# Gated delta-rule attention in a two-layer block on one NeuronCore: projections, solve, gated output and inverse steps placed anew within a loop step

## What is computed

```python
qkvz = hidden_states @ W_qkvz                 # per key head: q, k, 2 v, 2 z
conv = silu(sum(xp[:, j:j + Tv, :] * conv_w[:, j] for j in range(4)))   # q, k, v
beta, alpha = sigmoid(b), exp(-exp(A_log) * softplus(a + dt_bias))
q = l2norm(q) * DK ** -0.5;  k = l2norm(k)
def step(S, inp):                             # S: 128 x 128 per value head
    S = S * a_t
    v_new = (v_t - k_t @ S) * b_t
    S = S + outer(k_t, v_new)
    return S, q_t @ S
og = o * silu(z)
og = og * rsqrt(mean(og * og) + 1e-6) * norm_weight
out = og @ W_out                              # added to x, scaled by a gate
```

## Time and profile before

| | |
|---|---|
| median of 3 runs | 1607.65 us (1607.57 to 1608.58) |
| profiled execution, its time | 1606.35 us |
| its span, first to last instruction | 1604.6 us |
| mean granted TensorE clock over the span | 0.844 |
| busy share of the span: PE, DVE, ACT, POOL | 82%, 59%, 50%, 43% |

### The profile page before, as it was taken

How to read it: one execution, slowest core, us unless ns; L and a number is a source line. 1 busy time by engine, 2 the same in 40 slices (tenths; PEclk the granted TensorE clock), 3 DMA queues, 4 the chain that set the end, 5 groups by cost and what they waited for, 6 DMA issues and landing times. The chain is left out here.

```text
span 1604.6 us, 29952 instructions
## 1 busy us (share of the span) xinstructions
PE 1322.6 (82%) x10580; PEld 1120.7 (70%) x10580; DVE 954.1 (59%) x2298; ACT 809.6 (50%) x2096; POOL 690.4 (43%) x1137
## 2 busy tenths in 40 slices
PE   4376889889898988989889798898877399799995
PEld 1265778778787877878778787787766245488883
DVE  2487577786867868677686777768121322343335
ACT  1333466666666666665665666666453130353431
POOL 0118466485665746657475664856440000100000
PEclk8577799999999999999999999999776599855556
DMA  3311312313122130211303122021020300000002
GB/s 107 96 29 37 82 30 65 69 27 87 28 67 41 52 90 20 73 35 60 88 13 82 30 65 72 23 56 29 16 52 1 116 17 0 1 1 1 1 0 82
DMA packets 145273, 73.87 MB, mean 46 GB/s; under 512 B 118708, under 2 KB 134596, under 8 KB 143076
## 3 DMA queue, kind: packets, MB, share of 16 engines
q1 hardware_dynamic: 145124, 71.96, 17.4%
HBM read 58.11 MB, written 13.78 MB: 45 GB/s over the span
## 5 line engine op out<-in xcount | busy, mean ns | idle before, releaser
L878 POOL TENSOR_TENSOR tmp<-Dm,Tn 64x31 f32<-64x31 f32 (+15 forms) x496 | 253.7, 511 | 139.1 <-DMA Dm<-blk_in_scratch 104.9
L881 POOL TENSOR_TENSOR Tn<-Tn,tmp 64x31 f32<-64x31 f32 (+15 forms) x496 | 276.0, 556 | 38.9
L727 DVE SCALAR_TENSOR_TENSOR cqk<-bank,cw,cqk 128x255 f32<-128x255 f32 (+2 forms) x384 | 155.4, 475 | 151.5 <-ACT cqk L588 151.5
L854 POOL TENSOR_TENSOR ro<-ss,mhalf 128x4 f32<-128x4 f32 x64 | 64.6, 1009 | 297.3 <-issue 223.4
L727 DVE SCALAR_TENSOR_TENSOR cv<-bank,cw,cv 128x255 f32<-128x255 f32 (+2 forms) x384 | 155.4, 475 | 30.3 <-ACT cv L588 30.2
L649 ACT ACTIVATE junk<-og 128x129 f32<-128x129 f32 x256 | 80.1, 313 | 166.1 <-DVE og L799 137.5
L522 PE MATMUL bank<-wo,OTs 128*128 128x256 f32 x512 | 156.4, 433 | 3.4 <-ACT OTs L678 3.4
L786 DVE SCALAR_TENSOR_TENSOR BP<-bank,cj,E 128x512 f32<-128x512 f32 (+1 forms) x256 | 142.8, 612 | 2.3
L380 PE MATMUL bank<-hh,wqk_hi 128*128 128x256 f32 x256 | 94.9, 371 | 26.3 <-DVE wqk_lo L745 17.4
L114 POOL TENSOR_SCALAR vare<-mv 128x8 f32<-128x8 f32 x4 | 1.0, 239 | 259.3 <-DVE mv L105 259.3
L522 PEld LDWEIGHTS bank<-wo,OTs 128*128 128x128 f32 x512 | 95.5, 207 | 23.8 <-ACT OTs L678 10.2
(11 more groups left out here) (206 smaller groups left out, 3726.4 us busy)
## 6 DMA issues: line engine op xcount, KB each, us to landing
alb<-alpha_scratch SPq DMA_DIRECT2D x8, 1024.0 KB, 6.2
rvz<-in_L_attn_W_qkvz SPq DMA_DIRECT2D x16, 512.0 KB, 5.9
x<-alpha_scratch SPq DMA_DIRECT2D x8, 1024.0 KB, 6.4
blk_in_scratch<-BP SPq DMA_DIRECT2D x512, 8.0 KB, 1.5
rqk<-in_L_attn_W_qkvz SPq DMA_DIRECT2D x16, 256.0 KB, 2.6
wo<-in_L_attn_W_out SPq DMA_DIRECT2D x16, 256.0 KB, 6.9
tinv_scratch<-Tn SPq DMA_DIRECT2D x32, 128.0 KB, 2.2
tinv_t_scratch<-Tt SPq DMA_DIRECT2D x32, 128.0 KB, 2.2
```

The lines of the kernel that those rows point to most:

```text
L727: nc.vector.scalar_tensor_tensor(dst[:, t, s:T], bk[:, t * T:(t + 1) * T - s], cw[p][:, first + t, TAPS - 1 - s:TAPS - s], dst[:, t, s:T], ...
L854: nc.gpsimd.tensor_tensor(ro[b % 2][:], ss[b % 2][:], mhalf[:, 0:4], ALU.pow).then_inc(sem("ro"), 1)
L878: pool_step_done(nc.gpsimd.tensor_tensor(t, Dm[:, j, j + 1:BLK].unsqueeze(2).broadcast_to([SLOTS, r, c]), Tn[:, j, 0:c].unsqueeze(1).broad ...
L881: pool_step_done(nc.gpsimd.tensor_tensor(Tn[:, j + 1:BLK, 0:c], Tn[:, j + 1:BLK, 0:c], t, ALU.subtract), kh * NTS + 2 * j + 4)
```

## The change

- Banks: `bank[0]` is only the q/k projection's, `bank[1]` the first Gram matrix's, `bank[2]` the second's, and v and z share `bank[3]`. `pe_v` now also waits for the silu of the z before it, `pe_z` for the convolution of the v before it. `pe_qk` waits only for the convolution before it.
- PE: a step begins with both halves of the q/k projection. In merge steps the second half of v and the transposes `pe_ot` lie between merge stages 0 and 1, and `pe_vt` between solves 1 and 2. In plain steps `pe_z` comes last.
- ACT: in plain steps `act_silu_z` and then `act_ss` of the step itself come last, and in `b` = 3 `act_turn` after them; in merge steps `act_ogn` comes ahead of merge copy 0, `act_ots` ahead of merge copy 1, and `act_silu_qk` ahead of `act_y` 0.
- DVE: the scans move from the end of a step to the start of the next one, ahead of `dve_scales`; in plain steps `dve_og` of the step itself ends the step.
- The splits move: q/k from `b` = 2 to 1, v/z from `b` = 3 to the next head's `b` = 0.
- POOL: the parts of the inverse are 4, 11, 6 and 10 pairs (before 5, 10, 10 and 6); `pool_ro` is issued at the end of its own step, which leaves its place among POOL's instructions as it was but for the parts' borders.
- The stretch ahead of the loop: z of a sequence moves one turn later, ahead of the next v; the first Gram matrices no longer borrow `bank[6]`.

```diff
-            bQK, bG2, bV, bZ, bVT, bF, bX, bO = bank
-            bG1, bOT, bU = bQK, bVT, bO
+            bQK, bG1, bG2, bV, bVT, bF, bX, bO = bank
+            bZ, bOT, bU = bV, bVT, bO
...
             def pe_qk
-                    if lead:
-                        wait(nc.tensor, "conv_qk", at(kh, b, 6))
-                    else:
-                        wait(nc.tensor, "bp", at(kh, b, 4, -2))
+                    wait(nc.tensor, "conv_qk", at(kh, b, 6))
...
             def pe_v
                     wait(nc.tensor, "conv_v", at(kh, b, 6))
+                    wait(nc.tensor, "silu_z", at(kh, b, 1))
...
             def pe_z
-                    wait(nc.tensor, "silu_z", at(kh, b, 1))
+                    wait(nc.tensor, "conv_v", at(kh, b, 6, 6))
...
             def pe_step
+                if qk:
+                    pe_qk(*qk, 0)
+                    pe_qk(*qk, 1)
                 if gram:
                     pe_gram0(*gram)
                     pe_gram1(*gram)
+                if merges(b):
+                    if vz:
+                        pe_v(*vz, 0)
+                    pe_merge(kh, p, b, 0)
+                    if vz:
+                        pe_v(*vz, 1)
+                    if last:
+                        pe_ot(*last, 2 * (now + 2))
+                    pe_merge(kh, p, b, 1)
+                    if last:
+                        pe_f(*last, 0)
+                    pe_merge(kh, p, b, 2)
+                    if last:
+                        pe_f(*last, 1)
+                    pe_merge(kh, p, b, 3)
+                    if vz:
+                        pe_z(*vz, 0)
                     pe_solve(kh, p, b, 0)
+                    if vz:
+                        pe_z(*vz, 1)
                     pe_solve(kh, p, b, 1)
+                    if vt:
+                        pe_vt(*vt, now)
                     pe_solve(kh, p, b, 2)
                     pe_o(kh, p, b, 0)
+                    pe_o(kh, p, b, 1)
+                else:
+                    pe_solve(kh, p, b, 0)
+                    if vt:
+                        pe_vt(*vt, now - 1)
+                    if vz:
+                        pe_v(*vz, 0)
+                    pe_solve(kh, p, b, 1)
+                    if vz:
+                        pe_v(*vz, 1)
+                    pe_ot(*last, 2 * (now + 3))
+                    pe_solve(kh, p, b, 2)
+                    pe_o(kh, p, b, 0)
+                    pe_f(*last, 0)
+                    pe_o(kh, p, b, 1)
+                    pe_f(*last, 1)
+                    if vz:
+                        pe_z(*vz, 0)
+                        pe_z(*vz, 1)
...
             def act_silu_z
                 wait(nc.scalar, "z_mm", at(kh, b, 1, 1))
+                wait(nc.scalar, "og", at(kh, b, 2, -6))
...
             def act_step
+                if last and merges(last[2]):
                     act_ss(*last)
...
+                    if qk:
+                        act_silu_qk(*qk)
+                    if vz:
+                        act_silu_z(*vz)
+                    act_ss(kh, p, b)
                 if b == B - 1 and exists(kh, b, 1):
                     act_turn(kh + 1)
...
             def splits
-                if b == 2 and exists(kh + 3, 0, 0):
+                if b == 1 and exists(kh + 3, 0, 0):
                     split_qk(kh + 3, 1 - p)
-                if b == 3 and exists(kh + 2, 0, 0):
-                    split_vz(kh + 2, p)
+                if b == 0 and kh and exists(kh + 1, 0, 0):
+                    split_vz(kh + 1, 1 - p)
...
             def dve_step
                 if gram:
+                    for n in range(2 * R):
+                        dve_scan(*gram, n)
                     dve_scales(*gram)
                     dve_bp(*gram, 0)
...
+                if merges(b):
                     dve_r2(kh, p, b)
-                if qk:
-                    for n in range(2 * R):
-                        dve_scan(*qk, n)
+                else:
+                    dve_og(kh, p, b)
...
-            SPLIT = {0: (0, 5), 1: (5, 15), 2: (15, 25), 3: (25, BLK - 1)}
+            SPLIT = ((0, 4), (4, 15), (15, 21), (21, BLK - 1))
```

More of the change, by code:

```diff
@@ L389, in pe_gram0 @@
                 wait(nc.tensor, "bp", at(kh, b, 4))
-                nc.tensor.matmul(g1[:], sqk[i][:, 1, 0:P], sqk[i][:].rearrange("p x t -> p (x t)"), start=True, stop=True)
+                nc.tensor.matmul(bG1[:], sqk[i][:, 1, 0:P], sqk[i][:].rearrange("p x t -> p (x t)"), start=True, stop=True)
             def pe_gram1(kh, p, b):
@@ L503, in pe_o, with pe_ot @@
                 last.then_inc(sem("o"), 1)
-            def pe_ot(kh, p, b):
+            def pe_ot(kh, p, b, scaled):
                 wait(nc.tensor, "ogn", at(kh, b, 4, 4))
-                v = at(kh, b, 2, 8)
-                wait(nc.tensor, "vs", min(v, 2 * NG) if isinstance(v, int) else v)
+                wait(nc.tensor, "vs", min(scaled, 2 * NG))
                 for h in range(R):
@@ L554, in pe_step @@
[L554 to L569, removed]
@@ L696, in act_step @@
-                if last:
-                    act_ogn(*last)
-                if merge:
-                    act_merge(kh, p, b, 1)
-                if last:
-                    act_ots(*last)
                 if qk:
                     act_tap0(*qk, "qk", bQK, cqk, 0)
-                if merge:
+                if merges(b):
+                    if last:
+                        act_ogn(*last)
+                    act_merge(kh, p, b, 0)
+                    if vz:
+                        act_tap0(*vz, "v", bV, cv, 2)
+                    if last:
+                        act_ots(*last)
+                    act_merge(kh, p, b, 1)
+                    if vz:
+                        act_silu_v(*vz)
@@ L715, in act_step @@
-                if merge:
+                    if vz:
+                        act_silu_z(*vz)
                     act_y(kh, p, b, 1)
+                    if vt:
+                        act_vs(*vt)
+                else:
+                    act_y(kh, p, b, 0)
+                    if vt:
+                        act_vs(*vt)
+                    act_ogn(*last)
+                    if vz:
+                        act_tap0(*vz, "v", bV, cv, 2)
+                    act_y(kh, p, b, 1)
+                    act_ots(*last)
+                    if vz:
+                        act_silu_v(*vz)
+                    if qk:
+                        act_silu_qk(*qk)
+                    if vz:
+                        act_silu_z(*vz)
+                    act_ss(kh, p, b)
@@ L884, in pool_step @@
             def pool_step(kh, p, b):
-                last = beside(kh, p, b, -1)
-                if last:
-                    pool_ro(*last)
                 if kh + 1 < NKH:
@@ L892, in pool_step @@
                     pool_inverse(kh + 1, *SPLIT[b])
+                pool_ro(kh, p, b)
             def sp_load_qk(kh):
@@ L1085, in _ @@
                         for c in range(NC):
-                            dve_bp(gk, gk, gb, c, bX)
-                    for n in range(2 * R):
-                        dve_scan(kh, kh, b, n)
+                            dve_bp(gk, gk, gb, c)
+                    if g < LEAD_GRAM:
+                        for n in range(2 * R):
+                            dve_scan(kh, kh, b, n)
                     if 0 <= g - B < LEAD_VZ:
```

88 lines of the change are left out of this document (25 added, 63 removed).

## The result

The changed kernel takes 1679.97 us, median of 4 runs (1678.01 to 1682.1), against 1607.61 (1604.98 to 1608.58, 4 runs) for the kernel before in the same comparison: a ratio of 1.0446, 95% interval 1.0431 to 1.0461. The forecast was 1670, slower, range 1605 to 1715. The profiled execution has a span of 1676.3 us at a mean granted clock of 0.80.

A forecast was written before the change was run, and what follows sets the result against it. PE bounds step `b` = 1; `b` = 0 loses most, waiting at merge stage 0. Steps of 26.8 + 17.8 + 14.0 + 14.0 = 72.6 against 68.2: 4.4 a head, 14 heads, 62 us, so 1670; range 1605 to 1715.

The forecast's parts named there:

- The turn and the merge: ACT's turn starts 2.65 us into `b` = 0, merge stage 0 at 10.7; PE waits 6.2 us there.
- The 6.07 from the turn's end to the merge: In `b` = 0, time from ACT's turn ending to merge stage 0, kept from before because SP's order isn't changed.
- POOL isn't the limit: Claim that POOL's inverse, ending 0.8 us into the next head's first step, doesn't hold back the turn: cost 0.
- Plain steps: The two steps without merges: 12.7 us of work and 1.3 of waits, 14.0 each, a gain of 1.3 for both.
- The waits that I named: PE's waits in a plain step: 0.5 us for `ogn` at `pe_ot`, 0.8 for `OTs` at `pe_f` 0.
- the q/k term: PE's q/k projection at the step's start: 1.6 us a pair, 0.80 a half, taken equal to v's.
- Merge steps: From merge stage 0 on 13.3 us against 12.39; `b` = 1 takes 17.8, a loss of 1.3.
- Clock in `b` = 0: Lower clock behind the merge adds 2.8 us to 13.3; the step takes 26.8, a loss of 4.4.
- the bound of 5.6 from head 14: Upper bound of the clock term in `b` = 0, from head 14's first step: 18.9 us, 5.6 over 13.3.
- low-clock rival: Rival: the stretch after the merge behaves as in head 14, 2.8 us more a head, 1709 us; chance 0.15.
- Banks, scans, splits, ends: Bank sharing by v and z, moved scans and splits, stretch ahead of the loop, last two heads: each costed at 0.
- its 2.16 for the clock: Time the kernel before loses to the low clock in `b` = 0, from the merge on: 14.55 against 12.39 us.

The follow-up runs named there:

- e1: The changed kernel with ACT's turn moved ahead of the silu of z and the sums of squares in `b` = 3: 1645.80 us.
- e2: The changed kernel with the turn ahead of silu and square of q/k, and POOL's parts 4, 11, 8, 8 pairs: 1560.96 us.
- e4: The kernel before with the turn moved behind the sums of squares of the next head's first step: 1687.29 us.
- e10: The changed kernel with v's second half done seven times more (42 matmuls, results unused) in PE's wait ahead of merge stage 0 in `b` = 0: 1607.04 us.
- e11: e9 with v's second half done twice more (12 matmuls, results written over) ahead of merge stage 0 in `b` = 0: 1502.17 us.
- e7: The changed kernel with POOL's inverse in parts of 5, 10, 10 and 6 pairs again: 1678.68 us.
- e5: e8 with the second q/k half behind merge stage 1 in merge steps, and ACT's tap of q/k behind merge copy 1: 1554.56 us.
- e6: The changed kernel with 12 more matmuls of the q/k projection's shape behind merge stage 0 in `b` = 0, results unused: 1636.52 us.
- e9: e8 with POOL's parts 5, 12, 8 and 6 pairs: 1556.15 us.
- e8: e2 with `Y` ahead of silu of q/k and of z in merge steps, and `OTs` ahead of the second `Y` in plain steps: 1563.02 us.

## Why the prediction was right, and which of its sizes were not

- *The turn and the merge* (right, shown by e1, e2 and e4). Forecast: turn at 2.65, merge at 10.7, a wait of 6.2. Measured: 2.74, 10.87 (mean 10.63), 6.37. The 6.07 from the turn's end to the merge was 6.13. The turn's own sum is written wrongly: 0.2 + 0.58 + 1.67 make 2.45, not 2.65. The silu of z started at 0.49 instead of 0.2, behind silu and square of q/k, and this hid the slip. That POOL isn't the limit held for after: its last pair ends 1.14 into the step (forecast 0.8), 1.6 ahead of the turn. But the room is small: in e1, with the turn at 1.70, it waits for POOL 1.12.
- *Plain steps* (direction right, size off by 2.0 a head). Forecast 14.0 each, measured 13.05 and 12.98. The waits that I named are there, and `Y` is in time, but they are 0.6 smaller together: `ogn` 0.22 for 0.5 and `OTs` 0.52 for 0.8. The other 0.4 is PE's work: I took 12.7 from the busy time of before, and it is 12.3. Part of it is in the q/k term: I took 0.80 a half from the v half, and 12 q/k matmuls in a row, right behind z of the same shape, take 1.44 (652.44 to 653.88).
- *Merge steps* (size nearly right). `b` = 1: forecast 17.8, measured 17.45. That is near by two errors against each other: the waits for `Y` and `R2` of 0.45 and 0.35 are not there (under 0.1), and PE is idle 0.59 instead of 1.55, but it is busy 16.86, where I had taken 16.25. From the merge on at full clock I had 13.3; e10 shows 12.95.
- *Clock in* `b` = 0 (mis-sized). Forecast 2.8 over 13.3; measured 19.22 - 12.95 = 6.3. I had the bound of 5.6 from head 14 and chose against it, because v half 1 stays behind stage 0. This head's 18.86 is the 18.9 of the low-clock rival. The total came out near the forecast (72.6 a head, measured 73.3) only because the plain steps gave 2.0 back, and that is luck; the rival's time of 1709 would have needed them at 14.0.
- *Banks, scans, splits, ends* (costed at 0). PE has no wait for the silu of z or the taps of v in the head shown, and one of 0.8 for the silu of z in the whole loop. Of the 71.7 between the two profiled spans, 13 heads make 68.2; the last two heads take 1.4 more, the rest of the program, whose code is the same, 4.5 more, and what lies ahead of the 13 heads 2.4 less.

So where did the 5.1 us a head go? e10 gives the change at full clock, in the head that starts at 359.90: 10.64 + 12.95 + 17.44 + 13.05 + 12.99 = 67.1. The kernel before without its 2.16 for the clock would be 68.2 - 2.2 = 66.0. The order of the work, with the longer wait in it, costs 1.0 a head (`b` = 0 3.3 and `b` = 1 1.0 more, plain steps 3.3 less), and the clock 6.3 - 2.2 = 4.1. Four fifths of the loss are the clock, and the late turn starts it.

The Trainium skill, "TensorE: Matmul & The Clock Gate" (HAM oscillation — how this bites in real kernels), describes a loop whose matmuls wait for a DMA, so that each burst starts at the low clock. The trace agrees: with the wait filled, 9 of 13 heads of e10 ran 12.95 and 12 of 13 of e11 12.70, at a clock of 1.00. The Trainium skill, on the same page (Part 1: The HAM clock gate), says that activity releases the throttle. Here the trace disagrees: in after PE was busy 18.76 of 18.86 us and the mean clock was 0.59.

## What to carry to other kernels

Where an engine of fixed order issues a long-latency chain, place that instruction first and move everything else around it: here its place was worth 5% of the kernel before (e4) and, with two of POOL's pairs moved, 7% of the kernel after (e2). Cost a longer wait of TensorE at the idle time plus the slower clock behind it, which was the larger part here, and ask whether independent or even repeated matmuls can fill the wait. When a shortened step brings nothing, look for the engine whose chain now closes the head (here POOL), and for what stands in the queue behind the instruction that waits for it.

## What the runs showed of the hardware

- The low clock holds while PE works: 19.44 of 19.47 us busy at a mean clock of 0.56 in e7.
- Waits of only 1.5 to 2.1 us can be followed by the low clock: in e2 the same stretch took 12.94, 13.93 or 19.37 us.
- In e5 the clock fell behind a wait of 2.07 us at the Gram, with no wait at the merge, and stayed down 20.5 us in four heads.
- Adding matmuls made a kernel faster three times: 12 behind the merge 43 us (e6), 42 in the wait 73 us (e10), and 12 in e11's wait 54 us against e9.
- The same instructions behind the same wait give either length within one execution (14.51 and 19.47 in e7, 14.51 and 18.76 in e1), and e9 ran at a lower mean clock than e8, with a Gram wait less. What decides between them is not settled; that both the idle time (e4, e10, e11) and the work behind it (e6) move the odds is shown, a rule that gives the length is not.
